# The max pass of an attention kernel runs 17 rows ahead of the exponentials' blocks, where it ran 16 ahead

## The chip, the cores and the metric

The kernel runs on one core of a Trainium2 chip, in one launch. The metric is the device time in microseconds (us); lower is better. The core's engines run side by side, each through its own instruction stream in order, and meet at semaphores: TensorE (PE in the profile; PEld is its weight load), VectorE (DVE), ScalarE (ACT), GpSimd (POOL) and SyncE (SP), which here only issues DMA transfers.

## The reference

```python
x = layernorm(x + attention(x))          # 2 x 1024 x 128, 16 heads of 8
x = layernorm(x + block(x))

def attention(x):
    qkv = x @ qkv_w.T + qkv_b
    scores = einsum('bhid,bhjd->bhij', q, k) / sqrt(8) + alibi_bias   # 1024 x 1024 a head
    attn = softmax(scores)                                          # exp(s - row maximum) / sum
    return (attn @ v) @ out_w.T + out_b
```

`block` is a layernorm, a second, causal attention over two positions, a second layernorm, and a mixture of 8 experts with two experts for each of 2048 tokens. The change touches only the first attention; the rest follows it.

## The kernel before, in words

**Units and rows.** The first attention is cut into `UNITS` = 32 units. A unit m is two heads of one sequence with 512 queries each. It has two passes of `NB` = 8 rows. A row of the *max pass* (`max_half`, twice) is 128 queries against all 1024 keys, two matmuls of 512 columns into one of two pairs of PSUM banks; DVE then takes the maximum of each query (`reduce_row`, line 1215). A row j of the *exponential pass* (`exp_half`, twice) is a block of 128 keys against the 512 queries of each of the two heads; ACT takes the exponential (line 1068). Both write through `scores` (line 780; line 783 adds the bias on the diagonal). After four rows `values` (line 822) multiplies probabilities by v, one group of four rows late.

**What the second pass needs of the first.** The exponential pass has the maxima as three more rows of its stack of queries. To get there, the 8 maxima of a unit go through POOL (`split_max`, lines 541 to 547: three bf16 parts), DVE (`swap_max`, line 1223: a transpose), and SP (`load_max`): a write to memory (line 395), a wait for it, and a read back into the stack (line 397), which raises `max_loaded`.

**The stacks.** Queries and keys of a unit stand in one of four slots (`m % SLOTS`). SP loads unit m + 3 in its turn m (`load_tables`, `load_parts`: lines 372 to 387, five or six transfers, 528 KB), once the last exponential block of unit m - 1 is computed, since the slot was that unit's; the transfers raise `loaded`. Behind the loads in the same turn SP runs `load_max(m + 1)`.

**The order on PE, which the change touches.** First there are two units of max rows with nothing between them but small work of the start (`first_work`), 16 rows. Then each row (m, j) of the exponentials is preceded by the max row (m + 2, j), so that the max pass is 16 rows ahead. At j = 0 PE waits for `max_loaded` of unit m and for `loaded` of unit m + 2. A max row k waits until DVE has reduced row k - 2. The last two units have exponentials alone.

**The order on DVE.** It reduces the rows in their order; at i = 2 of unit m it transposes the maxima of unit m + 1 (`swap_max`), and at the ends of groups of four rows it does what is due of the later stages (`late`: norms, the second attention's scores and so on), whose places are fixed by the table `AT`.

**The tail.** When the attention of a fourth of the tokens is done (eight units), its later stages are spread over the following units; those of the last fourth, the scatter to the experts, the experts and the last layernorm follow the last unit.

The text below names the place of the exponential row j of unit m as "(m, j)".

Of the kernel before, what the change touches and what calls it, by code (L numbers as in the profile page):

```python
# [18 lines left out]
NB = N // P  # L19
NT = S * NB  # L20
HALF = N // 2
QUARTER = N // 4
RING = 3
WIDE_RING = 7
TURN_COLS = 32
GROUP = 4
# [3 lines left out]
PARTS = 3  # L30
# [5 lines left out]
SLOTS = 4  # L36
# [12 lines left out]
UNITS = CHUNKS * UNITS_C  # L49
# [49 lines left out]
def hooks(half):  # L99

    for c in range(LAST):
        for stage in range(STAGES):
            if AT[c // PER_S].get(stage, HALVES) == half - HALVES_C * (c + 1):
                yield stage, c
# [26 lines left out]
def ring_of(n):  # L131

    return n % RING if n < WIDE else (n - WIDE + RING) % WIDE_RING

# [10 lines left out]
def loads_by(m):  # L145

    return sum(5 - 4 * (k == 0) + (k % UNITS_C < SLOTS) for k in range(m % SLOTS, m + 1, SLOTS))


def body(nc, t):  # L150

    with ExitStack() as ctx:
# [3 lines left out]
        def sem(name):  # L156
            return ctx.enter_context(nc.semaphore(name))
# [80 lines left out]
        ld_w, ld_bias, ld_const, ld_slopes = sem("ld_w"), sem("ld_bias"), sem("ld_const"), sem("ld_slopes")  # L238
# [4 lines left out]
        qk_ready, qf_ready, q1_ready, r1_ready, q2_ready, q3_ready = (  # L243
            sem("qk_ready"), sem("qf_ready"), sem("q1_ready"), sem("r1_ready"), sem("q2_ready"), sem("q3_ready"))
        rest_left, rest_middle, rest_low = sem("rest_left"), sem("rest_middle"), sem("rest_low")
        rest_saved, first_loaded = sem("rest_saved"), sem("first_loaded")
        loaded_direct = sem("loaded_direct")
        parts_saved = [sem(f"parts_saved{b}") for b in range(4)]
        v_ready, v_kept, v_zeros, v_ones = sem("v_ready"), sem("v_kept"), sem("v_zeros"), sem("v_ones")
        loaded = [sem(f"loaded{k}") for k in range(SLOTS)]  # L250
# [47 lines left out]
        def max_pair(k):  # L298

            first_bank = RING + 2 * (k % 2)  # L300
            return ps[:, first_bank:first_bank + 2, :]
# [3 lines left out]
        def turn_of(m):  # L305

            return m // SLOTS + 1
# [406 lines left out]
        def _(pe):  # L714
# [7 lines left out]
            def project(y):  # L722

                s, c, half = piece(y)
                g = s * 2 + half
                pe.matmul(ps[:, PIECE_BANK[y], :], w_t[:, c, :], x_t[:, g * 512:(g + 1) * 512],
                          start=True, stop=True).then_inc(qk_ready, 1)
# [32 lines left out]
            def first_work(i):  # L760

                if i in (3, 5, 7, 9):
                    y = 4 + (i - 3) // 2
                    if y == 4:
                        pe.wait_ge(qf_ready, 3)
                    if y in (5, 6, 7):
                        pe.wait_ge(v_kept, (1, 2, 4)[y - 5])
                    project(y)
                if i == 11:
                    pe.wait_ge(late_w, 48)  # L770
                    pe.wait_ge(wo_ordered, 1)
                    pe.wait_ge(qf_ready, 5)
                    pe.transpose(ps[:, LATE_BANK, 0:P], wo_order[:], ident[:])
                    for a in range(2):
                        pe.transpose(ps[:, LATE_BANK, (1 + a) * P:(2 + a) * P], wq_nat[:, a, :], ident[:])
                    pe.transpose(ps[:, LATE_BANK, 3 * P:4 * P], wp_nat[:], ident[:]).then_inc(late_turned, 1)

            def scores(out, lhs, rhs, m, e, blk, on_diagonal):

                mm = pe.matmul(out, lhs, rhs, start=True, stop=not on_diagonal)  # L780
                if on_diagonal:
                    a = P * (blk % 4)
                    mm = pe.matmul(out[:, a:a + P], slope_eye[:, head_of(m, e), :], distance[:], start=False, stop=True)  # L783
                return mm

            def max_half(m, i, h):

                k, slot, e = NB * m + i, m % SLOTS, i // 4
                if h == 0 and k >= 2:
                    pe.wait_ge(mx_used, k - 1)  # L790
                mm = scores(max_pair(k)[:, h, :], q_stacks[0:K_MAX, slot, P * i:P * (i + 1)],
                            k_stacks[0:K_MAX, slot, e, HALF * h:HALF * (h + 1)], m, e, i, (m // UNITS_C) % 2 == h)
                if h == 1:
                    mm.then_inc(mx_full, 1)

            def ring_bank(n):

                if RING <= n < WIDE:
                    pe.wait_ge(ring_read, n - RING + 1)
                elif n == WIDE:  # L800
                    pe.wait_ge(mx_used, NB * UNITS)
                elif n >= WIDE + WIDE_RING - RING:
                    pe.wait_ge(ring_read, max(WIDE, n - WIDE_RING + 1))
                return ps[:, ring_of(n), :]

            def exp_half(m, j, e):

                slot = m % SLOTS
                scores(ring_bank(EXP_PLACE[m, j, e]), k_stacks[0:K_EXP, slot, e, P * j:P * (j + 1)],
                       q_stacks[0:K_EXP, slot, HALF * e:HALF * (e + 1)], m, e, j,  # L810
                       (m // UNITS_C) % 2 == j // 4).then_inc(ring_full, 1)

            def values(m, group):

                for j in range(GROUP * group, GROUP * (group + 1)):
                    if j == 0:
                        pe.wait_ge(v_copied, m + 1)
                        if m % 2 == 0 and m >= 2:
                            pe.wait_ge(o_kept, m // 2)
                    pe.wait_ge(ring_read, EXP_PLACE[m, j, 1] + 1)  # L820
                    for c in range(4):
                        mm = pe.matmul(ps_o[32 * c:32 * c + 32, :], v_unit[:, m % SLOTS, j, c // 2, :],  # L822
                                       probs[:, (NB * m + j) % KEPT, QUARTER * c:QUARTER * (c + 1)],
                                       start=(m % 2 == 0 and j == 0), stop=(m % 2 == 1 and j == NB - 1),
                                       tile_position=(0, 32 * c))
                    mm.then_inc(pv_done, 1)
# [69 lines left out]
            pe.wait_ge(x_kept[3], 1)  # L896
            pe.wait_ge(first_loaded, 16 * 3 * PARTS)
            pe.wait_ge(loaded[0], 16 * TABLES)
            for m in range(2):
                if m == 1:  # L900
                    pe.wait_ge(loaded[1], 16 * loads_by(1))
                for i in range(NB):
                    if m == 0 and i == 1:
                        pe.wait_ge(qf_ready, 4)
                        pe.wait_ge(v_kept, 3)
                    if m == 0 and i == GROUP:
                        pe.wait_ge(loaded_direct, 16 * 3 * PARTS)
                    for h in range(2):
                        max_half(m, i, h)
                    first_work(NB * m + i)  # L910
            pe.wait_ge(ld_slopes, 16)
            pe.wait_ge(late_kept, 5)
            pe.wait_ge(qf_ready, 8)

            for m in range(UNITS):
                for group in range(2):
                    for stage, c in hooks(2 * m + group):
                        late(stage, c)
                    for j in range(GROUP * group, GROUP * (group + 1)):
                        if j == 0:  # L920
                            pe.wait_ge(max_loaded[m % SLOTS], 16 * turn_of(m))
                            if m + 2 < UNITS:
                                pe.wait_ge(loaded[(m + 2) % SLOTS], 16 * loads_by(m + 2))
                        if m + 2 < UNITS:
                            for h in range(2):
                                max_half(m + 2, j, h)
                        for e in range(2):
                            exp_half(m, j, e)
                    if group == 1:
                        values(m, 0)  # L930
                    elif m > 0:
                        values(m - 1, 1)
# [232 lines left out]
        def _(dve):  # L1165
# [46 lines left out]
            def reduce_row(m, i):  # L1212
                k = NB * m + i
                dve.wait_ge(mx_full, k + 1)
                dve.tensor_reduce(row_max[:, m % 2, i:i + 1], max_pair(k).rearrange("p a n -> p (a n)"),  # L1215
                                  AX.X, ALU.max).then_inc(mx_used, 1)
# [41 lines left out]
            def late(stage, c):  # L1258
# [86 lines left out]
                if stage == SLOT:  # L1345
# [9 lines left out]
                                      ALU.add).then_inc(slots_ready, 1)  # L1355
                    dve.wait_ge(slots_ready, c + 1)

            for m in range(-2, UNITS):
                for i in range(NB):
                    if m + 2 < UNITS:  # L1360
                        reduce_row(m + 2, i)
                    if i == 2 and 0 <= m + 1 < UNITS:
                        swap_max(m + 1)
                    if i % GROUP == GROUP - 1 and m >= 0:
                        for stage, c in hooks(2 * m + i // GROUP):
                            late(stage, c)
# [147 lines left out]
```

## Time and profile before

| | us |
|---|---|
| median of 3 timed runs | 635.33 (634.46 to 636.42) |
| the profiled execution, whole | 632.58 |
| its span, from first to last instruction | 630.7 |
| PE busy | 524.3 (83%) |
| DVE busy | 397.6 (63%) |
| ACT busy | 344.0 (55%) |
| POOL busy | 215.4 (34%) |

The profile is of one execution. Its span lies within its own time, with 1.9 us around it. The busy shares are averages over stages with different limits: the start to about 45 us, the attention's units to about 455 us, the tail behind them. The granted clock of PE over the span is 0.915 of full speed: full for nearly all of the attention's units, and half for much of the tail up to the experts.

### The profile page before, as it was taken

What the parts mean: (1) busy time and instruction counts of PE and PEld (TensorE: products, weight loads), DVE (VectorE), ACT (ScalarE), POOL (GpSimd) and SP (SyncE); (2) the same over time, 40 slices, a digit from 0 to 9 for tenths busy, and PEclk for the clock granted to TensorE, in tenths of its full rate; (3) what the DMA queues carried; (4) which work ended last, traced back from release to release, by engine and by line L of the source; (5) the groups of instructions that cost most, each with busy time, mean ns of one, the idle gap of its engine ahead of it and who ended that gap; (6) DMA issues with size and microseconds to landing.
All of it is one profiled execution on the core that took longest, in us unless ns stands there. A gap on an engine that the chain in (4) does not pass through costs nothing.

```text
span 630.7 us, 11471 instructions
## 1 busy us (share of the span) xinstructions
PE 524.3 (83%) x4355; PEld 286.0 (45%) x4355; DVE 397.6 (63%) x654; ACT 344.0 (55%) x669; POOL 215.4 (34%) x394
## 2 busy tenths in 40 slices
PE   6579999999999999999999999998913306999930
PEld 4234444444444545444454444444512305888720
DVE  2598777777988677898758799876074321232227
ACT  4147666676768667667767665776802101323304
POOL 4635643111034161036314004710415150445440
PEclk9699999999999999999999999999955556999985
DMA  6632352223223222212212122200101002434124
GB/s 154 165 86 83 69 140 82 78 95 101 93 68 100 75 95 88 85 49 68 66 41 63 40 79 72 66 23 2 41 11 34 0 17 65 130 98 128 50 92 127
DMA packets 46999, 47.61 MB, mean 75 GB/s; under 512 B 12941, under 2 KB 36671, under 8 KB 46946
## 3 DMA queue, kind: packets, MB, share of 16 engines
q1 hardware_dynamic: 38610, 31.68, 17.7%
q0 software_dynamic: 5488, 12.73, 6.8%
q10 hardware_dynamic: 2848, 2.49, 1.3%
q8 instruction: 33, 0.54, 0.4%
q14 instruction: 20, 0.16, 0.1%
HBM read 31.42 MB, written 16.06 MB: 75 GB/s over the span
## 4 chain that ended last, share of the span: by engine, by line
PE 70%; DVE 16%; DMA 6%; issue 2%; ACT 2%; POOL 2%; SPq 0%; ACTq 0%; POOLq 0%; DVEq 0%
PE ps L780 31%; PE ps L822 16%; DVE row_max L1215 7%; PE ps L953 6%; PE ps L965 5%; PE ps L783 4%; PE ps L848 2%; DMA k_stacks<-k_dram 1%; DMA max_dram<-max_turned 1%; DVE heads L1267 1%; DMA k_dram<-parts 1%; DVE x_tok L1420 1%; PE ps L866 1%; PE ps L836 1%; PE ps L942 1%
## 5 line engine op out<-in xcount | busy, mean ns | idle before, releaser
L1215 DVE TENSOR_REDUCE row_max<-ps 128x1 f32<-128x1024 f32 x256 | 296.8, 1212 | 86.9 <-PE ps L780 44.3
L1068 ACT ACTIVATE probs<-ps 128x512 f32<-128x512 f32 x512 | 268.0, 608 | 86.0 <-PE ps L783 46.6
L780 PE MATMUL ps<-k_stacks,q_stacks 96*128 96x512 bf16 x512 | 164.0, 388 | 13.9 <-DVE row_max L1215 6.1
L780 PE MATMUL ps<-q_stacks,k_stacks 99*128 99x512 bf16 x512 | 160.8, 381 | 1.6 <-ACT probs L1068 1.6
L822 PE MATMUL ps<-probs,v_unit 128*32 128x256 f32 x2048 | 123.6, 382 | 0.0
L783 PE MATMUL ps<-distance,slope_eye 128*128 128x128 bf16 x512 | 113.4, 221 | 0.0
L780 PEld LDWEIGHTS ps<-k_stacks,q_stacks 96*128 96x128 bf16 x512 | 43.8, 99 | 94.9 <-DVE row_max L1215 36.0
L822 PEld LDWEIGHTS ps<-probs,v_unit 128*32 128x32 f32 x2048 | 60.1, 109 | 53.6 <-ACT probs L1068 10.3
L780 PEld LDWEIGHTS ps<-q_stacks,k_stacks 99*128 99x128 bf16 x512 | 48.8, 98 | 50.3 <-ACT probs L1068 12.7
L783 PEld LDWEIGHTS ps<-distance,slope_eye 128*128 128x128 bf16 x512 | 50.5, 99 | 25.6 <-issue 2.1
L1136 ACT ACTIVATE probs<-ps 128x640 f32<-128x640 f32 x32 | 22.5, 704 | 67.8 <-PE ps L953 67.8
L705 POOL DMA_INDIRECT yt<-prod_mix,y_to x40 | 38.9, 972 | 50.3 <-DVE prod_mix L1389 40.3
L532 POOL COPY v_unit<-v_all 128x128 f32<-128x128 f32 x32 | 9.2, 295 | 135.8 <-PE ps L822 135.8
L541 POOL TENSOR_TENSOR max_parts<-row_max,no_bits 128x8 bf16<-128x8 f32 x32 | 6.6, 205 | 118.2 <-DVE row_max L1215 118.1
L669 POOL DMA_INDIRECT xd<-row_of,slot_u x32 | 32.0, 1000 | 20.6 <-issue 11.4
L953 PE MATMUL ps<-probs,w 128*128 128x320 f32 x128 | 38.0, 452 | 1.2 <-DVE probs L1377 1.2
L965 PE MATMUL ps<-w,probs 128*128 128x128 f32 x280 | 32.4, 275 | 0.0
L965 PEld LDWEIGHTS ps<-w,probs 128*128 128x128 f32 x280 | 31.8, 192 | 0.0
L1376 DVE COPY columns<-probs 128x10 f32<-128x10 f32 x8 | 1.3, 166 | 44.8 <-PE ps L942 44.8
L953 PEld LDWEIGHTS ps<-probs,w 128*128 128x128 f32 x128 | 23.9, 199 | 12.3 <-ACT probs L1136 3.3
L942 PE MATMUL ps<-ident,probs 128*128 128x128 f32 x40 | 6.3, 292 | 16.7 <-DMA probs<-xd 16.7
L1387 DVE CAST y_to<-columns 128x5 uint32<-128x5 f32 x7 | 1.2, 172 | 23.8 <-PE ps L965 23.8
(183 smaller groups left out, 411.4 us busy)
## 6 DMA issues: line engine op xcount, KB each, us to landing
k_stacks<-k_dram SPq DMA_DIRECT2D x62, 144.0 KB
q_stacks<-q_dram SPq DMA_DIRECT2D x62, 72.0 KB
k_stacks<-in_c_alibi_k SPq DMA_DIRECT2D x32, 96.0 KB
w<-in_w SPq DMA_DIRECT2D x12, 256.0 KB, 2.9
xd<-blank POOLq DMA_DIRECT2D x8, 325.0 KB, 2.7
probs<-xd SPq DMA_DIRECT2D x8, 325.0 KB, 3.7
out_dram<-out_t SPq DMA_DIRECT2D x16, 128.0 KB
yt<-zeros POOLq DMA_DIRECT2D x4, 512.0 KB, 3.0
```

Source lines behind the costliest of these rows:

```text
L669: pool.indirect_dma_start(out=xd, out_offset=bass.IndirectOffsetOnAxis(ap=slot_u[c][:, k, j:j + 1], axis=0), in_=row_of[k][:, TC * c + j, ...
L705: pool.indirect_dma_start(out=yt, out_offset=bass.IndirectOffsetOnAxis(ap=y_to[u][:, a:a + 1], axis=0), in_=y_out[u][:, a, :], in_offset=N ...
L780: mm = pe.matmul(out, lhs, rhs, start=True, stop=not on_diagonal)
L783: mm = pe.matmul(out[:, a:a + P], slope_eye[:, head_of(m, e), :], distance[:], start=False, stop=True)
L822: mm = pe.matmul(ps_o[32 * c:32 * c + 32, :], v_unit[:, m % SLOTS, j, c // 2, :], probs[:, (NB * m + j) % KEPT, QUARTER * c:QUARTER * (c + ...
L848: mm = pe.matmul(out[:, (j % 2) * QKV:(j % 2 + 1) * QKV], turned[:, b, j * P:(j + 1) * P], wq_t[:], start=True, stop=True)
L942: mm = pe.transpose(ps[:, a // 4, (a % 4) * P:(a % 4 + 1) * P], x_in[u][:, a, 0:D], ident[:])
L953: mm = pe.matmul(ps[:, 2 + 2 * (f % 2) + h, 0:CAP // 2], w1[u][:, f * P:(f + 1) * P], x_in_t[u][:, h * CAP // 2:(h + 1) * CAP // 2], start ...
L965: mm = pe.matmul(ps[:, 6 + a // 4, (a % 4) * P:(a % 4 + 1) * P], act_t[u][:, f, a * P:(a + 1) * P], w2[u][:, f, :], start=(f == 0 and a % ...
L1068: act.activation(probs[:, k % KEPT, HALF * e:HALF * (e + 1)], ps[:, ring_of(n), :], ACT.Exp).then_inc(ring_read, 1)
L1136: act.activation(act_t[u][:, f, :].rearrange("p (h n) -> p h n", h=2), ps[:, 2 + 2 * (f % 2):4 + 2 * (f % 2), 0:CAP // 2], ACT.Gelu).then_ ...
L1215: dve.tensor_reduce(row_max[:, m % 2, i:i + 1], max_pair(k).rearrange("p a n -> p (a n)"), AX.X, ALU.max).then_inc(mx_used, 1)
```

## The change

A constant `LEAD` = 17 is added. The max rows get one running number k = 8 m + i. PE computes rows 0 to 16 ahead of the first exponentials, and before the exponentials of (m, j) the row 8 m + j + 17, which is (m + 2, j + 1), or for j = 7 the first row of unit m + 3. The wait for a unit's load moves with that first row. DVE reduces one row ahead of its loop, and then in its loop the row 8 m + i + 17. No instruction is added or left out, apart from the place of waits.

```diff
+LEAD = 2 * NB + 1
...
-            for m in range(2):
-                if m == 1:
-                    pe.wait_ge(loaded[1], 16 * loads_by(1))
-                for i in range(NB):
...
-                    for h in range(2):
-                        max_half(m, i, h)
-                    first_work(NB * m + i)
-            pe.wait_ge(ld_slopes, 16)
+            def max_row(k):
+
+                m, i = k // NB, k % NB
+                if m > 0 and i == 0:
+                    pe.wait_ge(loaded[m % SLOTS], 16 * loads_by(m))
+                for h in range(2):
+                    max_half(m, i, h)
+
+            for k in range(LEAD):
...
+                if k == 2 * NB:
+                    pe.wait_ge(ld_slopes, 16)
...
+                max_row(k)
+                first_work(k)
...
                         if j == 0:
                             pe.wait_ge(max_loaded[m % SLOTS], 16 * turn_of(m))
-                            if m + 2 < UNITS:
-                                pe.wait_ge(loaded[(m + 2) % SLOTS], 16 * loads_by(m + 2))
-                        if m + 2 < UNITS:
-                            for h in range(2):
-                                max_half(m + 2, j, h)
+                        if NB * m + j + LEAD < NB * UNITS:
+                            max_row(NB * m + j + LEAD)
                         for e in range(2):
                             exp_half(m, j, e)
...
+            for k in range(LEAD - 2 * NB):
+                reduce_row(k // NB, k % NB)
             for m in range(-2, UNITS):
                 for i in range(NB):
-                    if m + 2 < UNITS:
-                        reduce_row(m + 2, i)
+                    k = NB * m + i + LEAD
+                    if k < NB * UNITS:
+                        reduce_row(k // NB, k % NB)
                     if i == 2 and 0 <= m + 1 < UNITS:
                         swap_max(m + 1)
```

## Rows read from the trace of the kernel before

**Rows 1.** The page: busy us of the engines, share of the span.

```profile
PE 524.3 (83%) x4355; PEld 286.0 (45%) x4355; DVE 397.6 (63%) x654; ACT 344.0 (55%) x669; POOL 215.4 (34%) x394
```

**Rows 2.** Stretches: us, busy by engine, PEclk, DMA share, GB/s.

```profile
45.73:49.14 3.41, 3.41 (x14) 1.49 (x13) 2.61 (x3) 1.39 (x3) 2.43 (x7) 0.50 0.26 70
49.14:57.50 8.36, 8.29 (x68) 3.56 (x66) 7.41 (x8) 7.21 (x14) 6.63 (x16) 1.00 0.27 86
...
57.50:69.70 12.20, 12.17 (x117) 5.64 (x113) 9.33 (x9) 8.39 (x16) 5.78 (x11) 1.00 0.22 64
```

**Rows 3.** DVE in order of time, start us, us; the first units.

```profile
37.10 3.49 DVE L1215 TENSOR_REDUCE row_max<-ps 128x1 f32<-128x1024 f32 x3 [0.23 <-PE ps L780]
40.50 0.20 DVE L1223 STREAM_TRANSPOSE max_turned<-max_parts 128x32 bf16<-128x32 bf16 x1
40.63 6.92 DVE L1215 TENSOR_REDUCE row_max<-ps 128x1 f32<-128x1024 f32 x6
48.35 1.23 DVE L1215 TENSOR_REDUCE row_max<-ps 128x1 f32<-128x1024 f32 x1 [0.80 <-PE ps L780]
```

**Rows 4.** PE in order of time, where the exponentials begin.

```profile
45.42 0.38 PE L780 MATMUL ps<-k_stacks,q_stacks 96*128 96x512 bf16 x1 [0.63 <-DVE row_max L1215]
...
46.08 0.63 PE L780 MATMUL ps<-q_stacks,k_stacks 99*128 99x512 bf16 x1
```

**Rows 5.** SP in order of time: the maxima's write and read back.

```profile
40.73 0.38 SPq L395 DMA_DIRECT2D max_dram<-max_turned  x1
42.70 0.74 SPq L397 DMA_DIRECT2D q_stacks<-max_dram  x1
...
74.03 0.36 SPq L395 DMA_DIRECT2D max_dram<-max_turned  x1
78.54 0.72 SPq L397 DMA_DIRECT2D q_stacks<-max_dram  x1
...
82.94 0.71 SPq L387 DMA_DIRECT2D k_stacks<-k_dram  x1
```

**Rows 6.** The chain of waits, start us, us; ahead of unit 4.

```profile
86.21 6.85 DMA max_dram<-max_turned
...
93.07 2.25 DMA q_stacks<-max_dram
```

**Rows 7.** The page's DMA issues: KB each, median us to landing.

```profile
max_dram<-max_turned SPq DMA_DIRECT2D x32, 8.0 KB, 2.6
```

**Rows 8.** PE in order of time: (2, 7), (3, 7), values, (4, 0).

```profile
78.98 0.39 PE L780 MATMUL ps<-k_stacks,q_stacks 96*128 96x512 bf16 x1
...
91.15 0.39 PE L780 MATMUL ps<-k_stacks,q_stacks 96*128 96x512 bf16 x1
...
92.18 1.93 PE L822 MATMUL ps<-probs,v_unit 128*32 128x256 f32 x32
95.37 0.39 PE L780 MATMUL ps<-k_stacks,q_stacks 96*128 96x512 bf16 x1 [1.25 <-DMA q_stacks<-max_dram]
```

**Rows 9.** SP's queue of transfers, 91.15 to 92.3 and 92.3 to 93.1: packets, MB.

```profile
q1 hardware_dynamic: 51, 0.06, 19.6%
...
q1 hardware_dynamic: 8, 0.00, 0.7%
```

**Rows 10.** The chain of waits from unit 29's second half.

```profile
427.95 4.62 DVE row_max L1215 x4
432.57 1.36 DVE prod_mix L1289 x4
...
439.52 0.66 PE ps L861 x4
```

**Rows 11.** Waits, 45.4 to 440 us: total, times, longest us.

```profile
POOL v_unit L532 <- PE ps L822: 135.8, 28, 7.2
POOL max_parts L541 <- DVE row_max L1215: 109.8, 23, 13.5
...
DVE max_turned L1223 <- POOL max_parts L547: 1.0, 2, 0.6
```

More of the change, by code:

```diff
@@ L898, in _ @@
             pe.wait_ge(loaded[0], 16 * TABLES)
-            for m in range(2):
-                if m == 1:
-                    pe.wait_ge(loaded[1], 16 * loads_by(1))
-                for i in range(NB):
[L903 to L907, printed above, removed]
-                    for h in range(2):
-                        max_half(m, i, h)
-                    first_work(NB * m + i)
-            pe.wait_ge(ld_slopes, 16)
+            def max_row(k):
[5 more added lines that the diff above has]
+            for k in range(LEAD):
+                if k == 1:
+                    pe.wait_ge(qf_ready, 4)
+                    pe.wait_ge(v_kept, 3)
+                if k == 2 * NB:
+                    pe.wait_ge(ld_slopes, 16)
+                if k == GROUP:
+                    pe.wait_ge(loaded_direct, 16 * 3 * PARTS)
+                max_row(k)
+                first_work(k)
             pe.wait_ge(late_kept, 5)
```

## The prediction

> **What bounds the kernel now.** I read the page first. PE is busy 83% of the span [rows 1]. One unit of the steady part takes 12.2 us, of which PE is busy 12.17 and DVE 9.33, at the full granted clock [rows 2]: between 50 and 427 us PE sets the pace, and the reader is to see that moving a row within a unit leaves PE's sum as it is. So the change can act only where something other than that sum decides: at the start, where the max rows run alone; where the new waits stand; and at the end, where max rows run out. For these I read the order of time on DVE, PE and SP around the first exponentials [rows 3 to 5], the chain of waits where it leaves PE for a transfer [rows 6, 8], and the chain of the last units [rows 10].
>
> **The steady part: nothing.** Before and after, every place (m, j) has one max row and two exponential blocks, and DVE reduces the row of that place at that place. Both orders shift by the same one row, so the distance between PE and DVE, two pairs of banks, is what it was, and the late stages follow the same places. POOL's `split_max` can begin a row earlier (at the row of place (m, 6) and not (m, 7)). POOL idles for that 109.8 us in 23 waits [rows 11], and what it does next, the copy of v, waits for PE another 135.8 us in 28 waits, so an earlier start is more idle time. DVE waited for POOL's split 1.0 us in 2 waits [rows 11]; that is the most that an earlier split could give. I count 0, because with so much waiting elsewhere, a split that is late is late through POOL's own earlier work in that turn, which does not move.
>
> **The start: +0.7 us.** Before, DVE reduces rows 8, 9, 10 from 37.10 and transposes the maxima of unit 0 at 40.50 [rows 3]. After, its loop has reduced row 11 as well when it comes to the transpose: one reduction of 6.92 / 6 = 1.15 us later, at 41.65. What is queued behind: SP's write, issued 40.73 before, now 41.9; its completion took 42.70 - 40.73 = 1.97 us [rows 5]; the read then lands 2.25 us after its issue, as the one at 93.07 did [rows 6]. Before that gives 44.95, after 46.1. Before, PE came to (0, 0) at 45.42, released by DVE's reduction of row 14 [rows 4]; the first exponentials start at 46.08. After, PE computes row 16 at 45.42 just the same, and then stands before (0, 0) with two waits: the maxima (46.1) and, for row 17, the reduction of row 15, which is the fifth of six from 40.63 and ends at 40.63 + 5 x 1.15 = 46.4 [rows 3]. So (0, 0) starts at 46.5, 1.1 us later. DVE had 0.80 us of idle time ahead of 48.35, waiting for PE: from (0, 0) on PE is late and not DVE, so the delay is passed on.
>
> Part of it comes back through the clock. The granted clock is 0.50, its lower level of 1.2 GHz, from 45.73 to 49.14, and full behind it; in these 3.41 us PE was busy all the time, after a stretch of max rows in which it waited for DVE at every row [rows 2, 4]. That stretch costs half of 3.41 = 1.7 us. If it stands at the same place after the change, PE has work in it only from 46.5, 2.64 us, which costs 1.3: 0.4 us is given back. The start is then 1.1 - 0.4 = +0.7. Bounds: 0.4 (if DVE's later backlog covers 0.3 of it too) and 1.8, if the clock gives nothing back and the maxima's write, now issued beside POOL's stores, takes 2.6 us in place of 1.97 (the median of the 32 writes [rows 7]). I take 0.7, from the rows at this very place.
>
> **The new wait: +0.4 us.** PE asks for the load of unit m + 3 at (m, 7), before the exponentials of that row, and no more at (m + 1, 0). Between the two lie the exponentials of (m, 7) and one `values`: from 91.15 to 94.04, 2.9 us [rows 8]. Behind the wait on PE are those blocks and that `values`, and for them wait ACT and in the end DVE. The loads are issued over about 3.5 us once unit m - 1 is through, and SP's write of the maxima follows them on the same queue, so its completion tells roughly when they were through. In unit 2 the write issued at 74.03 was complete by 78.54, and (2, 7) came at 78.98: 0.4 us to spare [rows 5, 8]. In unit 3 the last load was issued at 82.94 [rows 5], and the write behind it was complete only at 93.07 [rows 6]. (3, 7) came at 91.15. The queue still moved 51 packets of 0.06 MB, data of the loads, between 91.15 and 92.3, and behind that only 8 small ones [rows 9]. So PE will stand at (3, 7) until some point between 92.3 and 93.1; I take 92.9, a wait of 1.7 us. Then (4, 0) could start at 92.9 + 2.9 = 95.8. It started at 95.37 before, since PE waited there for the maxima, 1.25 us by the record [rows 8]. That wait is swallowed, and the net cost is 95.8 - 95.4 = +0.4 us; by the bounds 0 and +0.6. In units 2 and 3 the write took 4.5 and 6.85 us, against a median of 2.6 [rows 7]; for the other units I count 0.
>
> The Trainium skill speaks against this term. Its page "DMA: Bandwidth & Descriptors", section "Anatomy of one DMA", gives a transfer about 2 us and its bytes at 436 GB/s (a fit for transfers issued by GpSimd). As an estimate by that page the 528 KB of a unit take 3.2 us from the last issue, would be in place at 86.2, and the term would be 0 (sum -0.45 by it). The trace disagrees in unit 3: the queue is moving data 8 us after the last issue.
>
> **The end: -1.15 us.** The place (29, 7) loses its max row; before it had the last one. There the chain runs through DVE: four reductions from 427.95, then the second attention's scores at 432.57 and on to PE's transposes at 439.52 [rows 10]. After, three reductions stand there, and the scores begin 4.62 / 4 = 1.15 us earlier; their inputs are ready, for the chain comes to them from the reductions. Everything up to 439.52 follows by 1.15 us. If DVE were not the path there, PE would save its max matmuls alone, about half of what (3, 7) took with its exponentials, 92.18 - 91.15 = 1.03 us: 0.5 us [rows 8]. I take 1.15; the bounds are 0.5 and 1.2.
>
> **The sum.** 0.7 + 0.4 - 1.15 = -0.05 us, no change: 632.58 stays 632.5 for the profiled execution. The median of the runs shown is 2.75 us above that execution, so I set the difference on the median: 635.33 - 0.05 = 635.3 us. With all bounds on one side the sum goes from 0.4 + 0 - 1.2 - 1.0 = -1.8 to 1.8 + 0.6 - 0.5 = +1.9.
>
> **The rivals.**
>
> *Slower: the loads are late at row 7 in more than one unit.* The place is (m, 7), the price what the load is late by, since nothing behind it gives it back unless the next unit waits for its maxima. It decides once a load is later by more than the spare, which is 0.4 us in unit 2 [rows 5, 8]. For it: in units 0 to 4 POOL moves weights, tables and parts at the same time, and the write took 4.5 us in unit 2 and 6.85 in unit 3 [rows 5, 6]. If unit 2 is late by 1.7 as well, its own wait for maxima does not absorb it, and a second such unit costs the same: +1.7 to +3.4 on the forecast, 637.0 to 638.7. If PE's idle time then takes its clock down for another 3.41 us, 1.7 more. Against it: all triggers of these transfers shift with PE, so their distances stay. Chance 0.19.
>
> *Faster: the end gives its row and the start costs nothing.* The clock's low stretch of 1.7 us [rows 2] would not come, or would fall into PE's waits ahead of 46.5, and DVE's 1.0 us of waits for the split [rows 11] would go. That is -0.05 - 1.3 - 1.0 = -2.4: 632.9. Against it: PE waits in the start for one row longer, which is more of what it did before its clock fell. Chance 0.12.
>
> *The change only moves time.* As forecast, but with other sizes at the three places: 633.5 to 637.2. Chance 0.69, with the forecast in it.
>
> **How the numbers follow.** About 0.3%, or 1.9 us, is what a measurement of this kernel can tell from no change. The forecast's case lies within it nearly whole: 0.67 of its 0.69, and 0.01 on either side. With the rivals: faster 0.12 + 0.01 = 0.13; within 0.3%: 0.67; slower 0.19 + 0.01 = 0.20. The range takes the bounds of the sum, 633.5 to 637.2, and goes on to the slower rival's first price and some way past it, and a little to the faster side: 633.4 to 638.2.
>
> **What would show it.** The first transpose of maxima (line 1223) at about 41.7, and the first exponential matmul at about 47.2. A wait of PE at line 780 before (3, 7) for a load of `k_stacks`, of 1 to 2 us, and none before (4, 0). Three reductions in one go before the scores of line 1289, not four. If PE shows waits for `k_stacks` loads in many units, the slower rival is right. If unit to unit times in the steady part differ from 12.2 us by more than 0.1, my claim that the steady part is untouched is wrong. If the low clock does not stand at about 45.7 to 49.1 in the start, the term of the start is wrong by up to 1.7 us.

## The result and the profile after

| | before | after |
|---|---|---|
| median of the runs, us | 635.05 (634.46 to 636.42, 6 runs) | 639.95 (637.34 to 642.09, 6 runs) |
| ratio, 95% interval | | 1.0072 [1.005, 1.0093] |
| profiled execution; its span | 632.58; 630.7 | 639.30; 637.4 |

The change makes the kernel 0.7% slower, 4.9 us. The forecast was no change, 635.3 within 633.4 to 638.2; the time lies outside.

The page after, the line that answers to [rows 1], and PE's clock in 40 slices:

```profile
PE 528.7 (83%) x4355; PEld 286.7 (45%) x4355; DVE 398.1 (62%) x654; ACT 344.3 (54%) x669; POOL 215.5 (34%) x394
...
PEclk9789999999999999999999999999955557999975
```

PE computes the same matmuls and is busy 4.4 us longer. To see where, I read on PE, in order of time, the start of the first weight load for the exponentials of some places (for row 8, of its own first weight load), and take the stages between them. They start at row 8 of the start, since up to there the profiles differ by up to 1.9 us though the code is the same (row 8 begins at 36.39 before, at 34.53 after: a load lands earlier or later). "Low" is time at the lower clock.

| stage, us | before | after | difference |
|---|---|---|---|
| row 8 to (1, 0) | 21.42, low 3.41 | 23.55, low 6.82 | +2.13 |
| (1, 0) to (4, 0) | 37.85 | 39.72, low 2.9 | +1.87 |
| (4, 0) to (27, 0) | 299.38 | 301.18 | +1.80 |
| unit 27 | 12.15 | 13.36 | +1.21 |
| (28, 0) to (31, 0) | 37.87 | 36.77 | -1.10 |
| from (31, 0) on | 185.67 | 188.34 | +2.7 |

The last line is not the change's: the two other profiled kernels that keep the lead of 16 (e3 and e10 below) have 187.8 and 189.5 there. The rest sums to +5.9. The +1.80 of the 23 units from (4, 0) to (27, 0) has three parts: 0.32 in unit 4, whose first 0.5 us still lie in the low clock that began at 95 us; 0.44 in unit 19; and 0.00 to 0.08 in each of the others.

**The start.** DVE after, start us, us:

```profile
32.81 7.05 DVE L1218 TENSOR_REDUCE row_max<-ps 128x1 f32<-128x1024 f32 x6
39.77 0.20 DVE L1226 STREAM_TRANSPOSE max_turned<-max_parts 128x32 bf16<-128x32 bf16 x1
39.90 7.10 DVE L1218 TENSOR_REDUCE row_max<-ps 128x1 f32<-128x1024 f32 x6
47.80 1.23 DVE L1218 TENSOR_REDUCE row_max<-ps 128x1 f32<-128x1024 f32 x1 [0.80 <-PE ps L781]
49.83 1.23 DVE L1218 TENSOR_REDUCE row_max<-ps 128x1 f32<-128x1024 f32 x1 [0.80 <-PE ps L781]
```

Against [rows 3]: the transpose comes a reduction later, and DVE then waits 0.80 us for PE twice; before, its second wait was 0.28 us. PE, with (0, 0) from 44.62:

```profile
43.49 0.44 PE L781 MATMUL ps<-k_stacks,q_stacks 96*128 96x512 bf16 x1 [0.56 <-DVE row_max L1218]
...
44.62 0.59 PE L781 MATMUL ps<-k_stacks,q_stacks 96*128 96x512 bf16 x1 [0.15 <-DVE row_max L1218]
...
45.53 0.63 PE L781 MATMUL ps<-q_stacks,k_stacks 99*128 99x512 bf16 x1
```

The stretches after (us, busy by engine, PEclk, DMA share, GB/s), against [rows 2]:

```profile
34.53:43.67 9.14, 6.63 (x31) 2.68 (x32) 9.06 (x10) 3.54 (x9) 5.28 (x10) 1.00 0.26 77
43.67:50.49 6.82, 6.67 (x23) 2.81 (x22) 5.14 (x5) 2.39 (x5) 5.26 (x13) 0.50 0.29 80
...
94.87:98.28 3.41, 3.41 (x32) 1.29 (x21) 0.29 (x1) 0.36 (x1) 0.00 (x0) 0.50 0.32 76
```

The low stretch of the start has doubled, 6.82 us in place of 3.41, and there is a second one at 95 us.

**(3, 7) to (4, 0).** PE after, against [rows 8]:

```profile
93.23 0.39 PE L781 MATMUL ps<-k_stacks,q_stacks 96*128 96x512 bf16 x1 [1.69 <-DMA k_stacks<-k_dram]
...
94.26 3.10 PE L823 MATMUL ps<-probs,v_unit 128*32 128x256 f32 x32
97.29 0.61 PE L781 MATMUL ps<-k_stacks,q_stacks 96*128 96x512 bf16 x1
```

The forecast wait is there, 1.69 us. The `values` behind it takes 3.10 us for 1.93, since the clock has fallen. There is no wait ahead of (4, 0).

**Row 7 of every unit.** PE's weight loads of the max rows of (6, 6) and (6, 7), before and then after:

```profile
127.85 0.11 PEld L780 LDWEIGHTS ps<-k_stacks,q_stacks 96*128 96x128 bf16 x2 [0.32 <-DVE row_max L1215]
128.98 0.11 PEld L780 LDWEIGHTS ps<-k_stacks,q_stacks 96*128 96x128 bf16 x2 [0.19 <-DVE row_max L1215]
```

```profile
130.38 0.11 PEld L781 LDWEIGHTS ps<-k_stacks,q_stacks 96*128 96x128 bf16 x2 [0.32 <-DVE row_max L1218]
131.57 0.13 PEld L781 LDWEIGHTS ps<-k_stacks,q_stacks 96*128 96x128 bf16 x2 [0.26 <-issue]
```

1.13 us from row 6 to row 7 before, 1.19 after, and the idle time is no longer ended by DVE but by "issue". The trace after has 29 instructions more, all of them waits on PE, as many as there are places where a unit's first max row now stands at j = 7. A weight load carries one wait. The first row of a unit has two or three; what is over goes into a wait instruction ahead of it. At j = 0 that instruction held two waits and ran while `values` was still in work. At (m, 7) the wait for DVE's reduction was moved into it, and the weight load kept the wait for the transfers: DVE's release passes first one instruction and then the next.

**Unit 27.** ACT, POOL, and PE's and DVE's part in the first max row, after and then before:

```profile
398.49 0.98 POOL L670 DMA_INDIRECT xd<-row_of,slot_u  x1 [0.30 <-issue]
398.84 0.58 ACT L1100 COPY moved<-ps 128x512 f32<-128x512 f32 x1 [2.25 <-PE ps L837]
398.97 0.22 PE L784 MATMUL ps<-distance,slope_eye 128*128 128x128 bf16 x1
399.51 1.26 POOL L628 TENSOR_TENSOR hid<-x_tok,moved 128x512 f32<-128x512 f32 x1
400.38 2.35 DVE L1218 TENSOR_REDUCE row_max<-ps 128x1 f32<-128x1024 f32 x2 [3.72 <-PE ps L784]
400.42 2.06 ACT L1071 ACTIVATE probs<-ps 128x512 f32<-128x512 f32 x4 [0.99 <-PE ps L781]
```

```profile
394.81 0.58 ACT L1097 COPY moved<-ps 128x512 f32<-128x512 f32 x1 [2.14 <-PE ps L836]
395.04 0.22 PE L783 MATMUL ps<-distance,slope_eye 128*128 128x128 bf16 x1
395.30 2.36 DVE L1215 TENSOR_REDUCE row_max<-ps 128x1 f32<-128x1024 f32 x2 [2.49 <-PE ps L783]
395.51 2.06 ACT L1068 ACTIVATE probs<-ps 128x512 f32<-128x512 f32 x4
395.76 0.97 POOL L669 DMA_INDIRECT xd<-row_of,slot_u  x1 [0.30 <-issue]
396.73 1.31 POOL L627 TENSOR_TENSOR hid<-x_tok,moved 128x512 f32<-128x512 f32 x1
```

POOL's sum into `hid` waits for ACT's copy in either case. Before, POOL was still issuing scatters when the copy ended. After, its split came a row earlier, the scatters too, and the sum starts at once, and ACT stands 0.99 us ahead of its first exponential. But it is not ACT that is slow. DVE stands as well, and both are released by PE: the semaphore of the max row's last matmul, which starts at 398.97, is raised only 1.39 us later (before 0.23 us after the start at 395.04), and that of the first exponential block's matmul 1.36 us after its start (before 0.39). PE's signals for two rows arrive together between 400.36 and 400.51. The first of them was due at 399.2, before POOL's sum began at 399.51, so the sum cannot be what held it back.

**The end**, against [rows 10]: three reductions, then the scores.

```profile
433.11 3.49 DVE row_max L1218 x3
436.60 1.36 DVE prod_mix L1292 x4
...
443.56 0.66 PE ps L862 x4
```

### The profile page after: what moved, and what is told of

Its sections match the earlier page's. It is cut to its first block, busy times and chain, and to the rows that moved or that the text cites. A ratio compares the mean times of both kernels' runs of the same rounds, so it can differ in the third digit from the quotient of the medians.

```text
span 637.4 us, 11500 instructions
## 1 busy us (share of the span) xinstructions
PE 528.7 (83%) x4355; PEld 286.7 (45%) x4355; DVE 398.1 (62%) x654; ACT 344.3 (54%) x669; POOL 215.5 (34%) x394
## 4 chain that ended last, share of the span: by engine, by line
PE 69%; DVE 17%; DMA 6%; issue 2%; ACT 2%; POOL 1%; another core or an unknown queue 1%; SPq 1%; ACTq 0%; POOLq 0%; DVEq 0%
PE ps L781 31%; PE ps L823 16%; DVE row_max L1218 8%; PE ps L956 6%; PE ps L968 5%; PE ps L784 4%; DMA k_stacks<-k_dram 3%; PE ps L849 2%; DVE heads L1270 1%; DMA k_dram<-parts 1%; DVE x_tok L1426 1%; PE ps L867 1%; PE ps L837 1%; PE ps L945 1%; POOL xd L670 1%
## 5 line engine op out<-in xcount | busy, mean ns | idle before, releaser
L1071 ACT ACTIVATE probs<-ps 128x512 f32<-128x512 f32 x512 | 268.3, 607 | 92.3 <-PE ps L784 48.0
```

What stands on the lines that cost most here:

```text
L1071: act.activation(probs[:, k % KEPT, HALF * e:HALF * (e + 1)], ps[:, ring_of(n), :], ACT.Exp).then_inc(ring_read, 1)
```

## The experiments

All times are medians; "before" is the kernel before on the same chip in the same job. Its median was 634.92 us for e1 to e4, 635.46 for e5 to e8, 635.83 for e9 to e12. The changed kernel itself was not run again beside them; it lies 4.9 us over the 635.05 of its own job. So a run is compared with it below by what each has over its own "before". Changes of a microsecond are read from the stages of the profiles, and the medians say whether they hold.

**e1: the order of two waits.**

```diff
-                if h == 0 and k >= 2:
+                if h == 0 and k >= 2 and not (m > 0 and i == 0):
                     pe.wait_ge(mx_used, k - 1)
...
                 if m > 0 and i == 0:
+                    pe.wait_ge(mx_used, k - 1)
                     pe.wait_ge(loaded[m % SLOTS], 16 * loads_by(m))
```

> The changed kernel (lead 17), with one difference: ahead of a unit's first max row PE waits first for DVE's reduction (mx_used) and then for the unit's load, not the other way round. Theory A (a separate wait instruction for mx_used stands in front of the weight load at (m, 7), on the path from DVE's release to PE, and costs 0.07 us in each of 28 units): the separate instruction becomes the one for the load, which has long landed; 1.5 to 2.0 us faster than the changed kernel's 639.95, so about 638.1, and no step of 0.07 at row 7 between the units. Rival B (the whole loss comes of the start and of the late load at (3, 7)): 639.9, no difference.

Measured 637.62, ratio to before 1.0031 [1.0015, 1.0047]: 2.7 us over its before, 2.2 less than the changed kernel. (4, 0) to (27, 0) takes 299.34 us: all of the +1.80 is gone, though not all of it by the order of the waits. About 1.2 of it is row 7; 0.25 is the low clock in unit 4, which this execution does not have; 0.37 is the step in unit 19. From (6, 6) to (6, 7):

```profile
130.46 0.11 PEld L781 LDWEIGHTS ps<-k_stacks,q_stacks 96*128 96x128 bf16 x2 [0.32 <-DVE row_max L1219]
131.59 0.11 PEld L781 LDWEIGHTS ps<-k_stacks,q_stacks 96*128 96x128 bf16 x2 [0.19 <-DVE row_max L1219]
```

1.13 us again, and released by DVE. Theory A holds. Unit 27 takes 12.58 us here, +0.43 where the changed kernel has +1.21, with POOL's split as early as there. This profile shows one thing more: a wait at (3, 7) without a low clock behind it.

```profile
95.11 0.38 PE L781 MATMUL ps<-k_stacks,q_stacks 96*128 96x512 bf16 x1 [1.82 <-DMA k_stacks<-k_dram]
...
96.12 1.93 PE L823 MATMUL ps<-probs,v_unit 128*32 128x256 f32 x32
97.99 0.39 PE L781 MATMUL ps<-k_stacks,q_stacks 96*128 96x512 bf16 x1
```

(1, 0) to (4, 0) takes 38.30 here, 0.45 more than before: the +0.4 of the forecast.

**e2 and e3: the expert weights later, with a lead of 17 and of 16.**

```diff
-                if m in (2, 3):
-                    u = m - 2
+                if m in (18, 19):
+                    u = m - 18
```

> The changed kernel (lead 17), with the two pairs of expert weights that POOL fetches in its turns 2 and 3 fetched in turns 18 and 19. Theory A (the load of unit 6 is late at (3, 7) through these transfers; PE idles 1.7 us and its clock then stands at 0.50 for 3.4 us): no wait at (3, 7), no low clock near 95 us, and none at (4, 0) either: 1.7 + 1.7 us less than the changed kernel, 636.5. Rival B (the queue is late through SP's and POOL's other transfers, the tables and k_dram and q_dram stores): the wait stays over 1 us, 639.5 to 640.

> The kernel before (lead 16), with the same fetches in turns 18 and 19. The control for the run beside it. Theory A: only the 1.25 us wait at (4, 0) goes, 635.05 - 1.25 = 633.8. If the weights' move costs something of its own where it lands (units 18 and 19), 634 to 635.

e2 measured 636.86 (1.0032 [1.0016, 1.0047]), 1.9 us over its before, 3.0 less than the changed kernel; (1, 0) to (4, 0) takes 36.75 us, with no wait for a load or for maxima and no low clock. So the transfers of the weights are what made PE wait. That load was complete 7.7 us after the issue of its last transfer, against 9.9 with the weights beside it. e3 measured 634.64 (0.9997 [0.9981, 1.0013]): the wait at (4, 0) is gone (36.52 us for the same stage, -1.33), but (4, 0) to (27, 0) takes 0.39 more, all of it in unit 20, behind the place to which the weights have moved, and the median shows no gain. Its profile has no low clock in the start; row 8 to (1, 0) takes 20.06 us.

**e4: the extra row at (4, 0) and not in the start.**

```diff
+                        if NB * m + j == EXTRA:        # EXTRA = 32
+                            max_row(EXTRA + 2 * NB)
                         if j == 0:
                             pe.wait_ge(max_loaded[m % SLOTS], 16 * turn_of(m))
...
```

> Lead 16 until (4, 0), where PE computes one extra max row ahead of its wait for the maxima of unit 4, and lead 17 from there on; start and (3, 7) are as before the change. Theory A: the extra row lies in the 1.25 us wait at (4, 0) and costs 0 to 0.5; the end gives 1.1; the waits at row 7 in the 25 units from 4 to 28 cost 25 x 0.07 = 1.7: 635.05 + 0.3 - 1.1 + 1.7 = 636.0. Rival B (start and (3, 7) are the whole loss): 635.05 - 1.1 + 0.3 = 634.2. Rival C (a lead of 17 is worse everywhere, for another reason): 638 or more.

Measured 637.06 (1.0029 [1.0013, 1.0046]), 1.1 over A's number and far from B's. The start is that of before, 21.48 us. The row did not lie in a wait for nothing: in this execution the maxima came 1.3 us later, PE then waited 1.98 us for them, and the clock fell for 3.41 us. Units 5 to 26 and unit 27 are those of the changed kernel, row 7 and the two steps included.

**e5: POOL's split at the place of before.**

```diff
-                pool.wait_ge(mx_used, NB * m + NB)
+                pool.wait_ge(mx_used, min(NB * m + NB + 1, NB * UNITS))
```

> The changed kernel (lead 17), with POOL's split of a unit's maxima waiting for one reduction more than it needs, so that it starts at the row of the same place as before the change. In the profiles of lead 17 unit 27 takes 13.36 us against 12.15 before, ACT standing 0.99 us ahead of its first exponential beside POOL's sum into hid, which has moved ahead by what the split moved. Theory C (POOL's earlier split brings that sum beside ACT's step): unit 27 takes 12.2 us again, total 1.2 us under the changed kernel's. Rival D (it is the lead itself or chance): unit 27 stays at 13.3.

Unit 27 takes 12.21 us, as theory C has it, and a step of 0.36 us in unit 19 is gone too. The median is 639.27 (1.0051 [1.0031, 1.0071]), 3.8 us over its before, 1.1 less than the changed kernel, which by itself is within what separates two medians; the stage is what shows it. ACT no longer stands:

```profile
398.22 0.58 ACT L1100 COPY moved<-ps 128x512 f32<-128x512 f32 x1 [2.14 <-issue]
398.93 3.07 ACT L1071 ACTIVATE probs<-ps 128x512 f32<-128x512 f32 x6
399.10 0.97 POOL L670 DMA_INDIRECT xd<-row_of,slot_u  x1 [0.30 <-issue]
400.08 1.30 POOL L628 TENSOR_TENSOR hid<-x_tok,moved 128x512 f32<-128x512 f32 x1
```

The max row's semaphore is raised 0.23 us after its matmul's start again. So the earlier split is needed for the loss. It is not the whole condition: of the seven profiles with the early split, ACT stands 0.95 to 0.99 us in six and 0.26 us in e1; unit 27 costs +1.2 in five of them, +0.43 in e1 and +0.66 in e8; and e1 and e8 have no step in unit 19. Which of POOL's instructions matters is not shown, since e5 moves all that stand behind the split.

**e6: the transpose one row earlier** (`i == 1` for `i == 2`).

> The changed kernel (lead 17), with DVE's transpose of the maxima at i = 1 in place of i = 2, so that the first one comes after the reduction of row 10 again. Theory A (the exponentials start 1.27 us later, since (0, 0) waits for DVE's reduction of row 15): the transpose is at 40.5 again by the clock of before, but row 8 to the first exponential stays at 10.3 to 10.6 us against 9.31. Rival E (the late maxima delay the start): it falls to 9.3 to 9.5.

Measured 640.06 (1.0074 [1.0049, 1.0098]). Row 8 to the first exponential stays at 10.58 us. The maxima are not what the start waits for; DVE's reduction is.

**e7: a lead of 15.**

```diff
-LEAD = 2 * NB + 1
+LEAD = 2 * NB - 1
...
```

> The code of the change with a lead of 15 rows: the opposite step. Theory A: the start gets what 17 lost, 1.2 us and the low clock (row 8 to (1, 0) 18.9 to 20.2 us, against 21.42 before and 23.5 with 17); the end loses 1.15 (from (28, 0) to (31, 0) 39.0 against 37.87); the load is asked for at (m, 1), where it has landed in every unit; the separate wait instruction costs less than 0.07 there, as PE does not wait for DVE at row 1. 633.5 to 635. Rival F (the lead has one best value, 16, since the split has a row less time here): DVE waits for the split in most units and it is slower, 637 or more.

Measured 639.20 (1.0065 [1.004, 1.009]), 3.7 us over its before: a miss. The start behaved as theory A has it (8.10 us from row 8 to the first exponential, 20.22 to (1, 0) with 3.41 us low), and (1, 0) to (4, 0) lost nothing (37.56). But units 19 and 27 lose 1.5 and 1.6 us and (28, 0) to (31, 0) takes 39.86, 2.0 more than before where 1.15 was expected. In that last stage the chain shows what the short lead does: the last reduction now stands behind the scores, the split and the transpose behind it, and DVE's mixing behind those:

```profile
433.83 1.35 DVE prod_mix L1291 x4
...
436.93 1.23 DVE row_max L1217
...
439.29 0.21 DVE max_turned L1225
```

Rival F was not what happened either: DVE did not wait in most units. What is left is that the lead sets which late stages a row's work lies beside; for units 19 and 27 that is a supposition, not tested.

**e8: e1 and e2 together.**

> The changed kernel (lead 17) with both cures, the waits' order and the later weights. Theory A: the two gains add, 637.62 - 639.95 and 636.86 - 639.95, to 634.5; what is left over the kernel with lead 16 and later weights (634.64) is the start (+1.9) and unit 27 (+0.4 to 1.2) less the end (-1.1). Rival B: they overlap, 636.5.

Measured 635.61 (1.0003 [0.9983, 1.0022]): two of the parts taken away bring the time back to that of before. It lies 0.15 us over its before, against 4.9 for the changed kernel; the two gains, 2.2 and 3.0, add to within 0.4. e8 and e2 differ in the order of the waits alone: 299.79 against 300.90 us from (4, 0) to (27, 0), so the order is worth 1.1 us there.

**e9 and e10: PE kept busy in the start, with a lead of 17 and of 16.** Two matmuls more behind rows 12 and on, whose output nobody reads.

```diff
                 max_row(k)
                 first_work(k)
+                if k == FILL_FROM:                     # 12
+                    pe.wait_ge(qf_ready, 8)
+                if k >= FILL_FROM:
+                    for _ in range(2):
+                        pe.matmul(ps[:, 7, :], q_stacks[0:K_MAX, 0, 0:P], k_stacks[0:K_MAX, 0, 0, 0:HALF],
+                                  start=True, stop=True)
```

> The changed kernel (lead 17), with two more matmuls of 512 columns behind each of the max rows 12 to 16 of the start, into a bank that nobody reads then, so that PE is busy while it waits for DVE. They compute nothing that is used. Theory A (the low clock of 6.83 us in the start follows from PE's idle time in the max rows, and the extra row lengthens it): no low clock from row 12 on; row 8 to (1, 0) 20.0 to 21.0 us against 23.5; median 2 to 3 us under the changed kernel's 639.95. Rival G (the stretch is fixed by something else): 23.3 to 23.6, and the median unchanged.

> The kernel before (lead 16) with the same filler behind rows 12 to 15. Theory A: row 8 to (1, 0) 20.0 us against 21.42, as in the profile of lead 16 that had no low clock there; 1.0 to 1.5 us faster than before where the low clock came. Rival G: no difference.

The low clock is gone from both. The stretches of e9, from row 8:

```profile
35.50:47.10 11.60, 10.60 (x53) 4.34 (x54) 11.11 (x12) 3.54 (x10) 6.64 (x16) 1.00 0.27 79
47.10:56.80 9.70, 9.43 (x76) 4.03 (x74) 8.61 (x9) 8.19 (x16) 8.15 (x18) 1.00 0.33 95
```

Row 8 to (1, 0) takes 21.27 us with 17 rows and 20.06 with 16. So the extra row costs 1.21 by itself, and the low clock 23.55 - 21.27 = 2.3 with a lead of 17 against 21.42 - 20.06 = 1.4 with 16. The filler itself costs nothing there: e3, whose start has no low clock and no filler, also takes 20.06. e9 measured 638.68 (1.0037 [1.0017, 1.0057]), 2.9 us over its before, 2.0 less than the changed kernel, where 2 to 3 were expected; e10 634.71, 0.9974 [0.9953, 0.9996], 1.1 us under before.

**e11 and e12: built from the parts.** e11: lead 16 to (12, 0), one extra row there, 17 behind it; e1's order, e2's weights, e5's split. e12: as e11 with a lead of 15 in the start, one extra row at (1, 0), and the filler.

```diff
-LEAD = 2 * NB + 1
+FIRST_LEAD, STEPS = 15, (8, 96)          # e11: 16, (96,)
...
+def rows_at(at):
+    if at < 0:
+        return range(FIRST_LEAD)
+    ahead = FIRST_LEAD + sum(at >= step for step in STEPS)
+    first = at + ahead - (at in STEPS)
+    return range(min(first, NB * UNITS), min(at + ahead + 1, NB * UNITS))
...
```

> A lead of 16 to (12, 0), one extra max row there, 17 behind it, with the waits' order of e1, the later weights of e2 and the split of e5. Theory A: against before, the wait at (4, 0) goes (-1.3), the extra row costs PE its own 0.5, the end gives 1.1, and start, row 7 and unit 27 cost nothing: -1.9, 633.3. Rival C (17 costs something else along the way): 635 or more.

> As e11, and the start with a lead of 15 rows, an extra row at (1, 0), and the filler behind rows 12 to 14. Theory A: 1.2 us less in the start, 1.4 less for the low clock, 0.5 more for the row at (1, 0): 2.1 us below e11, 631.2.

e11 measured 635.74 (0.999 [0.9969, 1.0012]), the time of before where 1.9 less was expected. (4, 0) to (27, 0) takes 300.97, 1.2 more than in e3, so the extra row costs there what a reduction takes and not 0.5, and the end's 1.1 only pays for it. Two terms were not in its sum: the 0.4 us of the moved weights in unit 20, known from e3, and 0.6 us in the start, where PE waits 0.96 us at (0, 0) for the first unit's maxima. e12 measured 632.81, 0.9952 [0.9928, 0.9975]: 3.0 us under before and faster than both kernels, by less than the 4.0 that was expected. Its profile has row 8 to (1, 0) in 19.70 us with no low clock, (1, 0) to (4, 0) in 37.13, unit 27 in 12.16, and 36.74 from (28, 0) to (31, 0). The gain is not one of the lead of 17: the row at (12, 0) costs 1.1 and the end gives 1.1. It comes from the start, 1.7 us, and from the weights, 1.3 less 0.4; the extra row at (1, 0) costs 0.6.

## Why the prediction was wrong

**The end, -1.15:** right. -1.10 in the profile, three reductions ahead of the scores.

**The start, +0.7:** wrong by its clock term. The row cost 1.21 (e9 against e10), where 1.1 was forecast, by the mechanism forecast: (0, 0) waits for the reduction of row 15 (e6 excludes the maxima). But "if it stands at the same place after the change, PE has work in it only from 46.5 ... 0.4 us is given back" failed. The low stretch did not stay at 3.41 us; it was 6.82 or 6.83 in all six profiles that start with a lead of 17 and have no filler, and about 3.41 or nothing in those that start with 16 or 15. The extra row is one more row in which PE waits about half the time. That PE's waits bring the low clock about is shown by the filler, which removes it (e9, e10); that the extra row is what doubles it rests on this count of profiles. It is +0.9 in place of -0.4. The Trainium skill's page "TensorE: Matmul & The Clock Gate", section "A second HAM failure mode: psum-queue depth-cycling", says that short idle times of PE between groups of matmuls, as it goes round its PSUM banks, are enough to take the clock down. The traces agree: PE's waits for DVE ahead of the low stretch are 0.42 to 0.56 us each, and filling them removes it.

**The new wait, +0.4:** the mechanism and the size of the wait were right (1.7 forecast, 1.69 found; +0.45 net in e1). What was missing from the sum is the clock behind it, which I had priced at 1.7 and put into the slower rival alone, for a second late load. Five profiles have this wait, 1.34 to 1.82 us long: the clock fell behind it in those of the changed kernel and of e5, not in those of e1, e6 and e9. (In e4 it fell behind the wait of 1.98 us at (4, 0).) So it is part of the price in some executions, about 1.4 us in the one profiled, of which 0.25 lie in unit 4. The second late load that this rival was about did not come. My estimate of 3.2 us from the last issue, worked out by the Trainium skill's page "DMA: Bandwidth & Descriptors", section "Anatomy of one DMA", spoke against the term and did not hold for these transfers of SP: before the change this load was complete 9.9 us after its last issue, at 92.8, and the loads of later units 4.8 to 6.1 us after theirs.

**The steady part, 0:** wrong twice, and these terms, about 3.0 us, are the largest part of what was missed; this is the step of the prediction that failed, with the clock terms of the other two places. "Every place has one max row" was true of the work and not of the instructions: the moved wait changed which wait the weight load carries, up to 0.08 us in a unit, 1.2 us from (4, 0) to (27, 0) and about 1.4 in all (1.1 in the first of these stretches by e8 against e2). The sign of being wrong that I gave for this term, 0.1 us a unit, was too coarse: 0.08 stays below it and adds up. And "an earlier start is more idle time" was false for POOL's split in units 19 and 27, where POOL's next work is not the copy of v but late stages: with the split at its old place 0.4 and 1.2 us are gone (e5). I read the totals of POOL's waits, and not what POOL does in the units where it does not wait.

Together, in the profile: 2.1 + 1.9 + 1.8 + 1.2 - 1.1 = +5.9 us up to (31, 0), against 4.9 between the medians. The profiled execution is one of those with the low clock at 95 us.

**Open.** Why PE's signals in unit 27 come about 1 us late when POOL's split is a row earlier. From 398.93 to 400.32 the trace has only two updates of any semaphore, and none of the load's transfers, which are in flight; at least one update, that of ACT's copy, is missing from it. It does not say what holds the signals back, and no run takes POOL's scatters or the transfers away by themselves. What makes units 19 and 27 lose 1.5 and 1.6 us with a lead of 15. The share of executions in which the clock falls at 95 us.

## What to carry to other kernels

When a row or a wait is moved, count the instructions that its waits need at the new place, and look at what the engine is doing there: a wait that was covered by queued work costs its full time at a place where the engine is released by another one, and putting the long-satisfied wait last, so that it goes into the separate instruction, can make it free. A cost too small to see in one unit counts once it is repeated: compare sums over many units. Where PE waits a little in every step, price the clock as part of the step and not as a constant. Where one engine's work moves earlier, look in each late stage at what it then runs beside; a total of idle time does not say that this is free.

## What the runs showed of the hardware

- A separate wait instruction between DVE's release and PE's weight load costs 0.00 to 0.08 us a unit (1.1 us over 23 units, e2 against e8); the same instruction with a wait that has long been satisfied costs nothing measurable (-0.04 us over 23 units, e1 against before).
- In unit 27 after the change the semaphore of a max row was raised 1.39 us after the start of its last matmul. At the same place before it was 0.23 us, and nowhere before over 0.65. DVE and ACT stood for it. The view names PE as the releaser; only the time from PE's start to the semaphore shows that the signal was late.
- Useless matmuls made the kernel faster: with four times two of them behind the max rows of the start the clock stayed full there, and the kernel took 0.26% [0.04, 0.47] less (e10).
- Profiles in which the code of a part is the same differ by up to 2.0 us before row 8 (36.49 in e1, 34.53 in the changed kernel) and by up to 4.3 us behind (31, 0) (185.67 before, 189.93 in e5), so a single profile cannot show a change of one microsecond by its span. In between they agree better: (4, 0) to (27, 0) took 299.38 before and 299.39 in e10.
